# Full attention of a fused network: four PSUM banks for scores and two for maxima, scores three slots ahead

## What is computed

```
q = rope(x Wq + bq); k = rope(x Wk + bk); v = x Wv + bv
scores = q k^T / sqrt(16)            # 512 x 512 for each of 8 * 16 heads
attn   = softmax(scores)             # exp(scores - row maximum) / sum
res    = res + (attn v) Wo + bo      # x above is layernorm(res), res the residual stream
```

## Time and profile before

| | |
|---|---|
| three runs, us | 4502.03, 4507.12, 4533.18 (median 4507.12) |
| the profiled execution, us | 4518.29, its span 4516.5 |
| granted TensorE clock, mean | 0.912 |
| PE, DVE, ACT, POOL busy, share of the span | 84%, 63%, 42%, 35% |
| reductions to maxima (L2752) | 512, 334.8 us busy |
| exponentials (L2694) | 512, 273.8 us busy |
| scores and maxima matmuls (L2578, L2568) | 512 each, 236.1 and 238.8 us busy |

### The profile page before, as it was taken

The page is one execution under the profiler, slowest core; times in us unless marked ns, Lnnn a source line. Parts: engine busy times, 40 slices in busy tenths (PEclk is TensorE's granted clock), DMA queues, the critical chain, the costliest instruction groups (busy, mean ns, idle before and its releaser), DMA issues. The chain is left out here.

```text
span 4516.5 us, 59985 instructions
## 1 busy us (share of the span) xinstructions
PE 3778.8 (84%) x19225; PEld 2609.4 (58%) x19288; DVE 2862.9 (63%) x5340; ACT 1914.0 (42%) x3859; POOL 1565.2 (35%) x1463
## 2 busy tenths in 40 slices
PE   3888879799599999988898588876885888888898
PEld 2555558688488888877787244444663333333566
DVE  6566547556465555546565477877884565654788
ACT  2555544344355555453343444422221455545232
POOL 3556525444466655436443201100002333330000
PEclk8888879899799999999999789897997799987899
DMA  5889821455100000002455100000002444440000
GB/s 138 255 217 279 239 75 58 141 166 158 47 10 11 15 15 11 1 18 73 154 160 157 57 10 19 19 1 14 0 0 52 101 96 83 99 82 15 5 14 19
DMA packets 221650, 348.36 MB, mean 77 GB/s; under 512 B 34632, under 2 KB 126266, under 8 KB 215226
## 3 DMA queue, kind: packets, MB, share of 16 engines
q1 hardware_dynamic: 198714, 260.66, 19.4%
q0 software_dynamic: 22656, 84.24, 8.2%
HBM read 166.29 MB, written 169.87 MB: 74 GB/s over the span
## 5 line engine op out<-in xcount | busy, mean ns | idle before, releaser
L2752 DVE TENSOR_REDUCE ab_nmx<-banks 128x1 f32<-128x512 f32 x512 | 334.8, 685 | 227.6 <-PE banks L2568 226.8
L2694 ACT ACTIVATE ab_pt<-banks 128x512 f32<-128x512 f32 x512 | 273.8, 600 | 97.8 <-PE banks L2578 85.7
L1645 POOL TENSOR_TENSOR lb_pq<-lb_pq,lb_rr 128x512 f32<-128x512 f32 x192 | 203.9, 1066 | 306.8 <-DVE lb_rr L1524 303.8
L2578 PE MATMUL banks<-ab_qT,ab_kT 49*128 49x512 f32 x512 | 236.1, 511 | 57.6 <-ACT ab_pt L2694 51.3
L1399 ACT ACTIVATE lb_pq<-banks,lb_nmx 128x256 f32<-128x256 f32 x384 | 178.9, 471 | 220.3 <-DVE lb_nmx L1519 217.5
L2568 PE MATMUL banks<-ab_kT,ab_qT 48*128 48x512 f32 x512 | 238.8, 513 | 28.8 <-DMA ab_kT<-ab_spill 17.1
L2578 PEld LDWEIGHTS banks<-ab_qT,ab_kT 49*128 49x128 f32 x512 | 94.5, 200 | 279.2 <-ACT ab_pt L2694 157.6
L1519 DVE TENSOR_REDUCE lb_nmx<-banks 128x2 f32<-128x512 f32 x192 | 131.4, 685 | 185.3 <-PE banks L1251 184.3
L615 POOL DMA_INDIRECT mb_xi<-moe_ys,moe_b_place x64 | 64.3, 1004 | 386.9 <-DVE mb_uT L2026 338.8
L347 ACT ACTIVATE da_pt<-banks 128x512 f32<-128x512 f32 (+1 forms) x384 | 175.0, 535 | 22.2 <-PE banks L265 20.1
L2806 POOL DMA_DIRECT2D ab_kT<-in_ab_ones x4 | 2.1, 545 | 524.7 <-POOLq L2958 524.7
(11 more groups left out here) (559 smaller groups left out, 11476.9 us busy)
## 6 DMA issues: line engine op xcount, KB each, us to landing
moe_xs<-zero SPq DMA_DIRECT2D x71, 512.0 KB, 11.0
moe_ys<-zero SPq DMA_DIRECT2D x71, 512.0 KB, 10.9
moe_a_w_raw<-in_moe_w SPq DMA_DIRECT2D x48, 512.0 KB, 3.7
moe_b_w_raw<-in_moe_w SPq DMA_DIRECT2D x48, 512.0 KB, 3.7
da_spill<-da_hi SPq DMA_DIRECT2D x128, 128.0 KB, 2.4
ab_spill<-ab_hi SPq DMA_DIRECT2D x128, 128.0 KB, 2.4
da_qT<-da_spill POOLq DMA_DIRECT2D x32, 384.0 KB, 7.0
da_kT<-da_spill POOLq DMA_DIRECT2D x32, 384.0 KB, 9.8
```

The costliest lines, as they stand in the source:

```text
L1645: nc.gpsimd.tensor_tensor(pq[:, n % RING, :, :], pq[:, n % RING, :, :], bcast(rr[:, n % RING, :], 2, 2 * P), ALU.mult).then_inc(s_p, 1)
L2578: nc.tensor.matmul(ps[:, EXP_BANK + n % 3, :], kT[b % 2][r:r + AB_ROWS + 1, p, j * P:(j + 1) * P], qT[b % 2][r:r + AB_ROWS + 1, p, :], sta ...
L2694: nc.scalar.activation(pt[:, s % RING, :], ps[:, EXP_BANK + s % 3, :], ACT.Exp, scale=AB_D ** -0.5).then_inc(s_e, 1)
L2752: nc.vector.tensor_reduce(nmx[:, g % 2, col:col + 1], ps[:, MAX_BANK + n % 3, :], op=ALU.max, axis=AX.X, negate=True).then_inc(s_mx, 1)
```

## The change

The eight banks are divided anew: two for maxima (0 and 1), four for scores (2 to 5). The waits follow: scores of n wait for exponential n-4, maxima of n for reduction n-2. PE's slot s now issues scores(s + 3) in place of scores(s + 2). LEAD, RING, the odd jobs and their slots stay.

```diff
-    MAX_BANK, EXP_BANK, SUM_BANK, ODD_BANK = 0, 3, 6, 7
+    MAX_BANK, EXP_BANK, SUM_BANK, ODD_BANK = 0, 2, 6, 7
+    NMAX, NEXP = 2, 4
...
-                    if n >= 3:
-                        pe.wait_ge(s_mx, n - 2)
-                    nc.tensor.matmul(ps[:, MAX_BANK + n % 3, :], qT[b % 2][r:r + AB_ROWS, p, qt * P:(qt + 1) * P],
+                    if n >= NMAX:
+                        pe.wait_ge(s_mx, n - NMAX + 1)
+                    nc.tensor.matmul(ps[:, MAX_BANK + n % NMAX, :], qT[b % 2][r:r + AB_ROWS, p, qt * P:(qt + 1) * P],
...
-                    if n >= 3:
-                        pe.wait_ge(s_e, n - 2)
-                    nc.tensor.matmul(ps[:, EXP_BANK + n % 3, :], kT[b % 2][r:r + AB_ROWS + 1, p, j * P:(j + 1) * P],
+                    if n >= NEXP:
+                        pe.wait_ge(s_e, n - NEXP + 1)
+                    nc.tensor.matmul(ps[:, EXP_BANK + n % NEXP, :], kT[b % 2][r:r + AB_ROWS + 1, p, j * P:(j + 1) * P],
...
-                    if 0 <= s + 2 < NS:
-                        scores(s + 2)
+                    if 0 <= s + NEXP - 1 < NS:
+                        scores(s + NEXP - 1)
...
-                        nc.scalar.activation(pt[:, s % RING, :], ps[:, EXP_BANK + s % 3, :], ACT.Exp,
+                        nc.scalar.activation(pt[:, s % RING, :], ps[:, EXP_BANK + s % NEXP, :], ACT.Exp,
...
-                        nc.vector.tensor_reduce(nmx[:, g % 2, col:col + 1], ps[:, MAX_BANK + n % 3, :], op=ALU.max,
+                        nc.vector.tensor_reduce(nmx[:, g % 2, col:col + 1], ps[:, MAX_BANK + n % NMAX, :], op=ALU.max,
```

## The result

The changed kernel takes 4906.3 us (median; 4884.5 to 4915.3) against 4506.2 us before: a ratio of 1.088, 95% interval 1.085 to 1.091. The forecast was 4580 us, 1.6% slower. The direction held, the size did not: +400 us in place of +73.

The account below looks back on a forecast made before the run. PE was taken as the bound. Row groups (6.2) and maxima banks (5.6 us a sequence) gave 87 us; with -4, +2 and -9.5 for the tail, +76, rounded to +73: 4580 us, 8-in-10 range 4532 to 4612.

Parts of the forecast that it names:

- The lead frees nothing on PE: Main stretch: scores three slots ahead still wait for exponential s-1, so PE's waits on ACT stay; taken as 0.
- The row groups: A slot's scores and maxima now share 64 rows; full-height work waits a second stream, 26 x 0.24 = 6.2 us a sequence.
- The sum: All terms over the whole kernel: net +76 us, rounded down to +73, 4580 us; chance 0.64 for +50 to +90.
- Rival 3: PE's new stalls drop the clock for one more 3 us spell a sequence: +22, in all about +97, 4603; chance 0.13.
- Two banks for maxima: Maxima n waits for reduction n-2, holding up work behind it on PE: 5.6 us a sequence, plus 2 at the start.
- The tail: After the maxima end, the four-slot period falls from 4.07 to 3.0 us; nine groups gain 9.5 us.
- What would show it: Next profile's signs: full-height work 0.67 us after a pair, maxima wait some 40, exponential wait near 45, tail period near 3.0.

Follow-up runs that it names:

- run 1: The changed kernel with each slot's maxima taken for the other head of its pair, so scores and maxima use different row halves: 4589.0 us, 1.011.
- run 3: The changed kernel with two maxima banks, three scores banks and scores two slots ahead again: 4579.8 us, 1.010.
- run 4: run 3 with the maxima taken for the other head, so a slot's two matmuls share one row half: 4929.9 us, 1.087.
- run 2: The kernel before with the maxima taken for the other head, so a slot's two matmuls share the same 64 rows: 4827.5 us, 1.062.
- run 6: run 4 plus, in even slots between scores and maxima, one extra unread 512-column matmul on the idle row half: 4816.9 us, 1.062.
- run 11: The kernel before plus one extra matmul beside the scores in tail slots 477 to 509, on the idle row half: 4521.5 us, 0.9997.
- run 9: run 1 with the values moved ahead of the scores in their slot: 4521.6 us, 0.9985.
- run 10: run 3 with the values moved ahead of the scores in their slot: 4534.0 us, 1.0017.
- run 7: run 4 plus, in even slots, one extra unread matmul on the row half that scores and maxima already use: 4931.9 us, 1.090.

## Why the prediction was wrong, point by point

- **The lead frees nothing on PE: right.** Slot s waited for exponential s-1 before and after. In run 1 PE still waits 45.0 us for exponentials, against 48.8, in run 3 43.7, and runs 1 and 3, and run 4 and the changed kernel, are equal within their intervals.
- **The row groups: right in mechanism and in the size of a stream, and the step that failed.** A pair followed by full-height work takes 0.67 us at the upper level, the 0.43 + 0.24 of the sum. But "26 x 0.24 = 6.2 us a sequence" took the upper level for granted. The term was 46 us; the rows alone cost 6.2% (run 2, about 280 us; its main stretch is 304 us longer than before), and on top of two banks 7.6% (run 4 against run 3, 350 us). The sum took the clock as a property of the stretch, 0.93, when the change took away what held it up: two halves at once (the main stretches with them have clocks of 0.86 to 0.97, those without 0.54 to 0.60, and run 6, with them in every other slot, 0.66). At the lower level a second stream costs more (full-height work follows the pair after 1.15 us, and after 0.72 where the two run together, in run 1 from 3916.81 to 3917.53: 0.43 for the stream in place of 0.24), and all other work on PE slows with it, as the values do, from 1.06 to 1.93 us.
- **Rival 3, the clock: the right quantity, but not the cause of the loss.** It put the loss down to stalls of 1 to 2 us and priced it at one more spell of 3 us a sequence, 22 us. Run 1 has these stalls and a clock of 0.87; run 2 has no new ones and 0.58. For the stalls themselves its price was near what is seen (next point). That stalls bring the clock down was its assumption, and no run shows it; they can account for that small part at most: the records show PE busy for 9.16 us of 10 where the clock falls (4010 to 4020), and 10.00 of 10 while it stays low (4050 to 4060). The single cold spell in the earlier trace rows, where PE was "busy throughout", was the hint.
- **Two banks for maxima: the waits right where they can be checked, the sum in part by luck.** 5.6 us a sequence and 2 us at the start made 43; run 3's main stretch is 47.3 us longer than before, its first part 3.0, its ratio 1.010 is 46 us. In slots 53 to 57 of run 1 values follow values after 3.33 us (3897.95 to 3901.28), where it was 2.74 before and 3.58 was worked out for pairs on one half. Run 1's pairs lie apart, and the difference is just the stream of 0.24. From slot 53 to 65 it is 10.49 us (to 3908.44) against 9.85: +0.64, where the +1.4 held three such streams. Eight such streams are in the 5.6 in all; without them it comes to 3.7, and the 43 to some 29. The rest is the clock. By their granted clocks (with levels of 1.00 and 0.50, the share at the lower one is twice what the clock lacks to 1), run 3's main stretch has 0.22 x 651.5 = 143 us at the lower level, that before 0.14 x 604.2 = 85, and run 11's, with the same instructions as before, 0.08 x 586.0 = 47 and is 18.2 us shorter: about 0.5 us for each. So by this estimate, from single executions, some 28 of the 47 us are clock and 19 are waits; PE's two waits together grew by 13.6 us (43.7 and 27.8 against 48.8 and 9.1).
- **The tail: over a third.** 9.5 us were forecast; at a clock of 0.50, in run 1, it takes 33.5 us instead of 37.1, and 31.8 in the changed kernel, whose last groups are mostly at the upper level (0.56 over the tail, 0.87 from 4555 to 4560). The period is 3.43 to 3.49 us, not 3.0. PE and ACT of the changed kernel:

```profile
4541.93 1.93 PE L2590 MATMUL banks<-ab_pt,ab_vx 128*32 128x512 f32 x8
4543.79 1.70 PE L2579 MATMUL banks<-ab_qT,ab_kT 49*128 49x512 f32 x4
4543.99 2.21 ACT L2695 ACTIVATE ab_pt<-banks 128x512 f32<-128x512 f32 x4 [1.23 <-PE banks L2590]
4545.42 1.93 PE L2590 MATMUL banks<-ab_pt,ab_vx 128*32 128x512 f32 x8
```

  The exponential that must wait for the values starts at 4543.99, behind the values of 4541.93; the fourth scores matmul loads 0.71 later (4544.70), and full-height work follows after 0.72 more. Together with 1.86 for the values and 0.20 until the exponential starts that is 3.49. The sum had no wait for this exponential: it gave all four scores 2 x 0.43 + 0.29 = 1.15 behind the values, and they take 1.63.
- **What would show it:** the wait for maxima was to grow to some 40 us (27.8) and that for exponentials to stay near 45 (15.2; 45.0 in run 1). The exponentials go with the clock: that wait is 13.7 to 16.5 us in the stretches at 0.54 to 0.58 (the changed kernel, runs 2 and 4) and 43.7 to 48.8 in those at 0.87 to 0.93 (before, runs 1 and 3). At the lower level PE is later, the values taking 1.93 us and not 1.06, and ACT's lateness no longer shows. The maxima do not: in runs 1 and 3, mostly at the upper level, that wait is 24.6 and 27.8 as well, so 40 was too high.

## What to carry to other kernels

When matmuls use part of the array's rows, look at which neighbours in PE's order lie in different row groups; a shift of one slot in one of two interleaved sequences can turn every pair of neighbours that runs together into one that does not. Price such a change at both levels of the clock, because here the array's use is what kept the clock up: the same-half streams came to 46 us by the sum at the upper level, and the measured cost was 280 to 350 with the level they brought about (a clock of 0.58 in run 2 against 0.93 before, 0.54 in run 4 against 0.89 in run 3). A term that comes out right may be two errors: split what was measured into waits, streams and clock before calling it confirmed. A bank, or a slot of lead, helps only if the wait in question moves with it: write out which event each slot waits for before and after, and if it is the same one, the buffer buys nothing.

## What the runs showed of the hardware that was not expected

- PE's clock averaged 0.54 over 995 us with PE's records busy for 95% of them, and 0.87 to 0.97 with 87 to 91% busy (runs 1, 3, 9 and 10). Here the busy share did not tell the clock.
- More matmuls made the kernel faster: 239 on the idle half, 2.5 points of ratio less (run 6 against run 4); as many on the busy half cost nothing that shows (run 7). A part of either may be waits that they filled.
- One and the same piece of program can run at either level: the tail of run 3 has the instructions and the order of the kernel before, and took 26.0 us at 0.93, there 37.1 at 0.50. What decides it no run shows. The main stretch, too, went from 604.2 to 586.0 us unchanged (before and run 11).
